# Attended values turned by products with a picking matrix, experts chosen by integer comparison from PSUM

## What is computed

```python
y = state_space_mixer(layernorm(x))                  # chunks, 4 heads, gate, rms norm
x = layernorm(x + (x + y @ W_out))
q, k, v = (x @ Wq.T + bq), (ctx @ Wk.T + bk), (ctx @ Wv.T + bv)   # 16 heads of 8
atten = softmax(q k^T / sqrt(8));  x = layernorm(x + (atten v) @ Wo.T + bo)
logits = x @ gate;  w, e = top_k(logits, 2)          # 8 experts
x = layernorm(x + sum_k softmax(w)_k * (silu(x @ w0[e_k]) * (x @ w1[e_k])) @ wo[e_k])
```

## Time and profile before

| | |
|---|---|
| median of 3 runs | 509.08 us (508.83 to 510.47) |
| the profiled execution | 508.15 us, span of its instructions 506.8 us |
| granted TensorE clock, mean | 0.748 |
| busy PE / DVE / ACT / POOL | 377.8 / 304.8 / 227.5 / 244.4 us |
| span by parts | front and mixer to 80 us, attention to some 302, its tail and the table to 338, experts to 484, end to 507 |

### The profile page before, as it was taken

One profiled execution on the slowest core, in us unless ns is written; L12 is line 12 of the kernel. 1 busy time (PEld: TensorE's weight loads), 2 busy tenths in 40 slices (PEclk: granted clock), 3 DMA queues, 4 the chain that ended last, 5 costly groups with the idle time before them and its releaser, 6 DMA issues.

```text
span 506.8 us, 7843 instructions
## 1 busy us (share of the span) xinstructions
PE 377.8 (75%) x2473; PEld 254.6 (50%) x2473; DVE 304.8 (60%) x778; ACT 227.5 (45%) x455; POOL 244.4 (48%) x309
## 2 busy tenths in 40 slices
PE   3997687877898788787576968218997898888900
PEld 1765555554444465443233424116886687676800
DVE  2655346786768878888987374413545455364635
ACT  2775544124656654646373732013534354353504
POOL 3723676443333415135566665534564555553316
PEclk9997557555759886957675555557899899998975
DMA  8731316355040404161232310011111111111052
GB/s 289 279 107 63 95 52 174 87 137 156 25 136 4 126 4 126 35 179 57 63 118 63 119 42 13 12 53 36 33 43 32 40 39 38 41 32 33 22 181 84
DMA packets 40312, 41.42 MB, mean 82 GB/s; under 512 B 5041, under 2 KB 34033, under 8 KB 40273
## 3 DMA queue, kind: packets, MB, share of 16 engines
q1 hardware_dynamic: 35888, 34.06, 22.2%
q0 software_dynamic: 3520, 5.25, 3.9%
q10 hardware_dynamic: 864, 1.61, 0.9%
HBM read 26.91 MB, written 13.73 MB: 80 GB/s over the span
## 4 chain that ended last, share of the span: by engine, by line
PE 48%; DVE 23%; issue 8%; POOL 6%; another core or an unknown queue 5%; ACT 5%; DMA 3%; DVEq 0%; ACTq 0%; POOLq 0%; SPq 0%
PE banks L886 9%; DVE nm L1079 7%; PE banks L794 4%; PE banks L746 4%; PE banks L909 4%; DVE topf L1141 3%; PE banks L694 3%; PE banks L617 3%; PE banks L714 2%; PE banks L898 2%; POOL table_dram L1553 2%; PE banks L737 1%; PE banks L910 1%; PE banks L704 1%
## 5 line engine op out<-in xcount | busy, mean ns | idle before, releaser
L1380 ACT ACTIVATE probs_all<-banks 128x1024 f32<-128x1024 f32 x64 | 65.5, 1023 | 67.7 <-PE banks L746 65.5
L1079 DVE TENSOR_REDUCE nm<-banks 128x4 f32<-128x1024 f32 x64 | 78.0, 1218 | 15.6 <-PE banks L737 14.5
L886 PE MATMUL banks<-w_split,scores_in 128*128 x234 | 68.5, 431 | 3.6 <-DVE scores_in L1223 2.8
L1578 POOL DMA_INDIRECT y_dram<-avT,scatter_u x39 | 38.2, 979 | 59.6 <-DVE avT L1229 53.5
L794 PE MATMUL banks<-probs_all,vals 128*9 128x256 f32 x512 | 55.2, 515 | 2.3 <-DVE avT L1095 1.2
L746 PE MATMUL banks<-scores_in 32*128 32x256 f32 x256 | 42.7, 420 | 16.6 <-DVE nm L1079 14.5
L1210 DVE TENSOR_TENSOR ctx_in<-ctx_in,banks 128x512 f32<-128x512 f32 x39 | 26.7, 684 | 41.1 <-issue 26.4
L886 PEld LDWEIGHTS banks<-w_split,scores_in 128*128 128x128 f32 x234 | 43.9, 203 | 13.5 <-issue 6.3
L909 PE MATMUL banks<-w_split,scores_in 128*128 x156 | 42.4, 349 | 8.1 <-DVE scores_in L1216 7.7
L737 PE MATMUL banks<-scores_in 32*128 32x256 f32 x256 | 42.4, 418 | 6.2 <-DVE nm L1079 6.0
L1571 POOL DMA_INDIRECT scores_in<-x_dram,gather_i x39 | 37.4, 959 | 18.0 <-issue 11.6
(11 more groups left out here) (212 smaller groups left out, 785.5 us busy)
## 6 DMA issues: line engine op xcount, KB each, us to landing
scores_in<-k_dram SPq DMA_DIRECT2D x32, 128.0 KB, 2.8
scores_in<-q_dram SPq DMA_DIRECT2D x32, 128.0 KB, 3.1
ctx_in<-in_L_ffn_w SPq DMA_DIRECT2D x16, 256.0 KB, 2.6
cs_wide<-cs_dram SPq DMA_DIRECT2D x14, 256.0 KB, 3.7
k_dram<-split_qk SPq DMA_DIRECT2D x8, 256.0 KB, 2.5
q_dram<-split_qk SPq DMA_DIRECT2D x8, 256.0 KB, 2.2
ctx_in<-in_L_ffn_wo SPq DMA_DIRECT2D x8, 256.0 KB, 2.8
x_in<-in_x SPq DMA_DIRECT2D x4, 256.0 KB, 5.2
```

Source lines behind the costliest of these rows:

```text
L886: m = TE.matmul(bank(2 * slot + j), xT[:, i % XT, xh, :], all_weights[:, c + j * FF:][:, bass.ds(expert_at[i], FF)], start=n == 0, stop=n ...
L1079: V.tensor_reduce(most, maxima_of(n).rearrange("p (j k q) -> p j k q", j=2, k=TPS), AX_X, ALU.max, negate=True).then_inc(s["nmax"], 1)
L1380: C.activation(probs(n).rearrange("p j k q -> p (j k q)"), EXPS, ACT.Exp, scale=SCALE).then_inc(s["probs"], 1)
L1578: G.indirect_dma_start(y_dram[:, :], bass.IndirectOffsetOnAxis(ap=scatter_u[:, i:i + 1], axis=0), y_slot[:, i % Y_RING, :], None).then_inc ...
```

## The change

1. `divide` is one stage for the whole batch: eight products with `pick` as moving operand (128x36, one column for each of 9 values of 4 heads) take the place of the eight transposes. Both halves, 2 x 16 heads x 9 values, stand densely in one bank, so DVE divides with one reciprocal of 128x32 and one product of 128x256. `turn_heads` and `out_project` move one step forward for the first six batches.
2. `gate_top`: a product of the identity with the numbers 0 to 7 writes them into the bank beside the logits. DVE compares the integer indices `topi` with that part of the bank; the cast to `topf` is gone. The bank is free with `chosen`, no longer with the copy of the logits.
3. The subtraction into `row_src` moves from DVE to GpSimd, as a stage `choose` of its own behind the wait for `top`.
4. The constant table `rest` gets 36 columns more.

```diff
@@ -73,8 +73,8 @@
 (IDENT, W_IN, LN_W, LN_B, DT_BIAS), N_FIRST = columns(P, DIN, 1, 1, NH)
 (W_K, W_V, B_Q, B_K, B_V), N_KV = columns(D, D, 1, 1, D)
 (ROPE_CS, W_O_MIX, A_LOG), N_MIX = columns(2 * TPS * 2 * ROPE, 2 * D, NH)
-(CAUSAL, BELOW, ABOVE, EXPERT_OFFSET, W_Q, W_O, B_O, D_SKIP, RMS_W, GATE, MASK, LIMIT, CODES, SPARE, IOTA), N_REST = columns(
-    P, P, P, P, D, D, D, NH, 2, NE, NE, 1, B * TOPK * TPS, SLOT_TILES, SLOT_TILES)
+(CAUSAL, BELOW, ABOVE, EXPERT_OFFSET, W_Q, W_O, B_O, D_SKIP, RMS_W, GATE, MASK, LIMIT, CODES, SPARE, IOTA, PICK), N_REST = columns(
+    P, P, P, P, D, D, D, NH, 2, NE, NE, 1, B * TOPK * TPS, SLOT_TILES, SLOT_TILES, GJ * (HD + 1))
 Y_RING = 6
 
 
@@ -158,13 +158,12 @@
     (lambda b: (("gate_top", b), ("choose", b)), 9),
     (whole("split_x2"), 8),
     (whole("x2_norm"), 7),
-    (whole("out_project"), 6),
-    (whole("turn_heads"), 5),
-    (half("divide", 1), 3),
-    (half("divide", 0), 2),
+    (whole("out_project"), 5),
+    (whole("turn_heads"), 4),
+    (whole("divide"), 2),
     (half("evacuate", 1), 0),
 )
-SOONER = (15, 9, 7, 6, 5, 4, 3, 2, 0)
+SOONER = (15, 9, 7, 6, 5, 4, 2, 0)
 BANKS_END = (2, 3)
 LAST_AFTER = 16
 LAST_MIXER = tile_step(NT - 1) + LAGS[0][1]
...
@@ -318,7 +317,6 @@
         logit = sb("logit", [P, TPS, NE])
         top = sb("top", [P, TPS, 8])
         topi = sb("topi", [P, TPS, 8], U32)
-        topf = sb("topf", [P, TPS, 8])
         choice = sb("choice", [P, TOPK, TPS, NE])
         chosen = sb("chosen", [P, TPS, NE], BF16)
         before_b = sb("before_b", [P, P], BF16)
@@ -455,11 +453,13 @@
         def maxima_of(n):
             return bank(6, 2) if second_slot(n) else MAXIMA
 
-        def follow_up(b, half=0):
-
-            if b < B - len(BANKS_END):
-                return MISC
-            return bank(0) if b == B - 1 and half else bank(BANKS_END[b - B])
+        def follow_up(b):
+
+            return MISC if b < B - len(BANKS_END) else bank(BANKS_END[b - B])
+
+        def by_head(b):
+
+            return follow_up(b)[:, 0:TPS * AH * (HD + 1)].rearrange("p (k h c) -> p k h c", k=TPS, c=HD + 1)
 
         def shared(i):
 
@@ -591,15 +591,11 @@
             misc, mix_bank = Bank(q), Bank(q)
             misc.freed_at(s["fall"], TURNED_SUMS)
             ends = [Bank(q) for _ in BANKS_END]
-            last_half = Bank(q)
             for e in ends:
                 e.freed_at(s["nmax"], NPAIR)
-            last_half.freed_at(s["probs"], NPAIR)
-
-            def freed(b, half=0):
-                if b < B - len(BANKS_END):
-                    return misc
-                return last_half if b == B - 1 and half else ends[b - B]
+
+            def freed(b):
+                return misc if b < B - len(BANKS_END) else ends[b - B]
 
             def turn_normed(t):
                 slot = t % 2
@@ -797,17 +793,19 @@
                 if k == 1:
                     m.then_inc(s["av_mm"], 1)
 
-            def divide(b, half):
+            def divide(b):
                 q.wait_ge(s["av_lo"], b + 1)
                 q.wait_ge(s["av_hi"], b + 1)
-                freed(b, half).wait()
-                for g in range(4):
-                    m = TE.transpose(follow_up(b, half)[:, g * P:(g + 1) * P], avT[:, g * S + half * P:g * S + (half + 1) * P], ident)
+                freed(b).wait()
+                for k in range(TPS):
+                    for r in range(GR):
+                        m = TE.matmul(by_head(b)[:, k].rearrange("p (j r) c -> p r j c", r=GR)[:, r],
+                                      avT[:, r * S + k * P:r * S + (k + 1) * P], pick, start=True, stop=True)
                 m.then_inc(s["heads_t"], 1)
-                freed(b, half).freed_at(s["o_norm"], TPS * b + half + 1)
+                freed(b).freed_at(s["o_norm"], b + 1)
 
             def turn_heads(b):
-                q.wait_ge(s["o_norm"], TPS * b + 2)
+                q.wait_ge(s["o_norm"], b + 1)
                 freed(b).wait()
                 for k in range(TPS):
                     m = TE.transpose(follow_up(b)[:, k * P:(k + 1) * P], o_sb[:, k, :], ident)
@@ -834,9 +832,10 @@
                 freed(b).wait()
                 q.wait_ge(s["x2T"], b + 1)
                 for k in range(TPS):
-                    m = TE.matmul(follow_up(b)[:, k * NE:(k + 1) * NE], x2T[:, k * P:(k + 1) * P], gate[:, :], start=True, stop=True)
-                m.then_inc(s["gate_mm"], 1)
-                freed(b).freed_at(s["logit"], b + 1)
+                    TE.matmul(follow_up(b)[:, k * NE:(k + 1) * NE], x2T[:, k * P:(k + 1) * P], gate[:, :], start=True, stop=True)
+                TE.matmul(follow_up(b)[:, TPS * NE:(TPS + 1) * NE], ident, iota[:, 0:NE],
+                          start=True, stop=True).then_inc(s["gate_mm"], 1)
+                freed(b).freed_at(s["chosen"], b + 1)
 
             def rank_chosen(b):
                 q.wait_ge(s["chosen"], b + 1)
@@ -1090,20 +1089,19 @@
             def evacuate(b, half):
                 if half:
                     q.wait_ge(s["av_mm"], GR * (b + 1))
-                    q.wait_ge(s["heads_t"], TPS * b)
+                    q.wait_ge(s["heads_t"], b)
                     q.wait_ge(a["init_dram"], INIT)
                     V.tensor_copy(avT[:, BANK:], AV).then_inc(s["av_hi"], 1)
 
-            def divide(b, half):
-                av = follow_up(b, half).rearrange("p (r j c) -> p r j c", r=GR, c=32)
-                q.wait_ge(s["heads_t"], TPS * b + half + 1)
-                q.wait_ge(s["o_norm"], TPS * b + half)
-                own.step(V.reciprocal(rec[:, :].rearrange("p (r j) -> p r j", r=GR), av[:, :, :, HD]))
+            def divide(b):
+                av = by_head(b).rearrange("p k h c -> p (k h) c")
+                q.wait_ge(s["heads_t"], b + 1)
+                q.wait_ge(s["o_norm"], b)
+                own.step(V.reciprocal(rec[:, :], av[:, :, HD]))
                 own.settle()
                 q.wait_ge(s["o_t"], b)
-                V.tensor_tensor(o_sb[:, half, :].rearrange("p (j r d) -> p r j d", r=GR, d=HD), av[:, :, :, 0:HD],
-                                rec[:, :].rearrange("p (r j) -> p r j", r=GR).unsqueeze(3).to_broadcast([P, GR, GJ, HD]),
-                                ALU.mult).then_inc(s["o_norm"], 1)
+                V.tensor_tensor(o_sb[:, :, :].rearrange("p k (h d) -> p (k h) d", d=HD), av[:, :, 0:HD],
+                                rec[:, :].unsqueeze(2).to_broadcast([P, TPS * AH, HD]), ALU.mult).then_inc(s["o_norm"], 1)
 
             def out_project(b):
                 q.wait_ge(s["wo_mm"], b + 1)
@@ -1127,24 +1125,20 @@
 
             def gate_top(b):
                 q.wait_ge(s["gate_mm"], b + 1)
-                V.tensor_copy(logit[:, :, :].rearrange("p t e -> p (t e)"), follow_up(b)[:, 0:TPS * NE]).then_inc(s["logit"], 1)
-                q.wait_ge(s["logit"], b + 1)
+                own.step(V.tensor_copy(logit[:, :, :].rearrange("p t e -> p (t e)"), follow_up(b)[:, 0:TPS * NE]))
+                own.settle()
+                q.wait_ge(s["gap"], b)
                 for k in range(TPS):
                     own.step(V.max(top[:, k, :], logit[:, k, :]))
                 own.settle()
                 for k in range(TPS):
-                    own.step(V.max_index(topi[:, k, :], top[:, k, :], logit[:, k, :]))
-                own.settle()
-                q.wait_ge(s["consts_g"], ROWS_SET)
-                V.tensor_tensor(row_src[:, b, :, :, 1], top[:, :, 1].unsqueeze(1).to_broadcast([P, TOPK, TPS]),
-                                top[:, :, 0].unsqueeze(1).to_broadcast([P, TOPK, TPS]), ALU.subtract).then_inc(s["gap"], 1)
-                own.step(V.tensor_copy(topf[:, :, :], topi[:, :, :]))
-                own.settle()
+                    V.max_index(topi[:, k, :], top[:, k, :], logit[:, k, :]).then_inc(s["top"], 1)
 
             def choose(b):
+                q.wait_ge(s["top"], TPS * (b + 1))
                 for k in range(TOPK):
-                    own.step(V.tensor_tensor(choice[:, k], iota[:, 0:NE].unsqueeze(1).to_broadcast([P, TPS, NE]),
-                                             topf[:, :, k].unsqueeze(2).to_broadcast([P, TPS, NE]), ALU.is_equal))
+                    own.step(V.tensor_tensor(choice[:, k], follow_up(b)[:, TPS * NE:(TPS + 1) * NE].unsqueeze(1).to_broadcast([P, TPS, NE]),
+                                             topi[:, :, k].unsqueeze(2).to_broadcast([P, TPS, NE]), ALU.is_equal))
                 own.settle()
                 q.wait_ge(s["rank_mm"], b)
                 V.tensor_tensor(chosen[:, :, :], choice[:, 0], choice[:, 1], ALU.add).then_inc(s["chosen"], 1)
@@ -1166,7 +1160,7 @@
             def place_chosen(b):
                 q.wait_ge(a[f"slots{b % 2}"], 16 * TOPK * TPS * (b // 2))
                 V.scalar_tensor_tensor(place_u[:, b % 2].rearrange("p (k t) -> p k t", k=TOPK),
-                                       topf[:, :, 0:TOPK].rearrange("p t k -> p k t"), float(T),
```

(8 more changed lines are left out.)

12 lines of the change are left out of this document (6 added, 6 removed).

## The result

The changed kernel is slower: 511.86 us (median of 4) against 508.95 for the kernel before beside it, ratio 1.0135 with a 95% interval of 1.0072 to 1.0198. On another chip it is 491.16 against 479.06, ratio 1.0257 (1.0207 to 1.0308). On most of them, as on that one, the part with the experts, behind 340 us, takes some 25 us less than on the first, in every kernel alike, while the stretch up to 300 us takes the same. So each time is compared only with the kernel before on its own chip, and kernels on different chips by their distance from it. One kernel's times spread with its granted clock (the change's own from 489.37 at 0.722 to 494.11 at 0.700), so medians have 1 to 3 us of play.

The account below looks back on a forecast made before the run. PE and DVE were taken to bound the middle part by turns, with three stalls. The terms 4.55 + 1.35 - 9.15 - 1.5 + 2.1 gave -2.65 us, so 506.4 us against 509.08, range 500 to 513.

Parts of the forecast that it names:

- rival 2: Divisions: products at half clock throughout, added PE work on the chain at that price, moved step brings nothing; 512.0 us, chance 0.22.
- Bound and stalls: Batches 3 to 5: PE's 14.4 us wait for `o_sb`, blamed on the cast, goes with cast and gaps; -9.15 us.
- Rival 1: Three stalls move to `chosen`, which loses at every border of POOL's row as the cast did; 524 us, chance 0.07.
- Price of the products: Each batch's division: sixteen passes at 0.225 us at half or 0.125 at full clock, so 3.6 or 2.0 us.
- Early divisions, +4.55: Divisions of b=0 to 3, before the stalls: products in place of transposes add 0.95, 0.85, 1.25 and 1.5 us.
- Extra product, +1.35: Gate of b=0, 1, 2: two more passes writing the experts' numbers, 0.45 us each at half clock; +1.35 us.
- Moved steps, -1.5: Turning and out-projection one step forward take DVE work from a late step, for b=3 and partly b=4; -1.5 us.
- Tail, +2.1: Chain through b=7 after the last scores: dearer products, gate of b=6, POOL's subtraction, less DVE time; +2.1 us.
- Rival 3: From about 270 us the full clock returns, where it had stayed at 0.50 to the attention's end; 497 us, chance 0.13.

Follow-up runs that it names:

- one stray copy: Kernel before with the change's routing, transposes kept, plus a copy of the indices directly behind `chosen`: ratio 1.0034; with the copy ahead of the comparisons instead: 1.0021.
- the pair of added products: Kernel before with new routing and moved steps, transposes kept, plus 32 products of 36 columns (481.28 us, ratio 1.0031) or of 128 columns (471.57 us, 0.9864).
- the transposing kernel: Kernel before with the change's routing, eight transposes kept: 468.46 us, ratio 0.975; with the moved steps as well: 463.54 us, ratio 0.9643.
- division alone: Changed kernel with the old routing (cast and gap subtraction on VectorE, choice from SBUF, no extra product): median 487.06 us, ratio 1.0059.
- the wide products: Kernel before with new routing and moved steps, transposes kept, plus two products of 128 columns ahead of each half's transposes: 471.57 us, ratio 0.9864.
- the doubled transposes: Kernel before with new routing and moved steps, each half's four transposes done a second time: 465.96 us, ratio 0.9741; on another chip 0.9663.
- the routing part: Kernel before with the choice from the bank, gaps on GpSimd and the gate's extra product, transposes kept: 468.46 against 479.45 us, ratio 0.975.
- the one-pass products: Changed kernel with the division's products reading only upper halves as bf16, one pass in place of four: 462.50 against 481.32 us, ratio 0.9614.

## Why the prediction was wrong

It said 506.4 us and faster; 511.86 lies in its range and on rival 2's 512.0, to which it gave 0.22. By its terms:

- **Bound and stalls.** The wait of 14.4 us was real, and is gone; -9.15 became -8.3. Its cause was only half told, and `chosen` was safe for another reason than mine: as the only such instruction in the row. Rival 1 was one stray copy away.
- **Price of the products.** 3.6 and 2.0 us for a division measured 3.63 and 1.98. This size was right. The reading behind it, that 8 columns cost as much as 64, set a price at half clock beside one at full; at half clock a pass took 0.21 us with 8 columns, 0.23 with 36 and 0.26 with 128 (2.05 us for eight).
- **Early divisions, +4.55: the step that failed.** It reads "the longer stretch of busy PE reaches the full clock", for b=1 and b=2. The clock did not come: it stayed at 0.50 from 174 to 186 us, though PE was busy for 11.6 of these 12 us, the projections behind the two divisions took 2.05 and 2.06 us where 0.91 was counted on, and the granted clock of 180 to 240 us fell from 0.78 to 0.64. The delay grew by 1.1, 3.3, 2.8 and 2.4 us in the steps of b=0 to 3, together 9.6, where 0.95, 0.85, 1.25 and 1.5 were forecast; the excess lies in b=1 and b=2. Step 42 is 9.1 us late where 4.55 + 1.35 - 1.5 = 4.4 was forecast. That the clock stayed away because the added work had few columns is inferred from the pair of added products; no run has the division itself with more columns.
- **Extra product, +1.35**: perhaps too small, but not settled. By the medians 4.6 us between the changed kernel and the same without it, and 2.6 in the transposing kernel, on different chips each time; exponential 42 is 9.1 us late with it and without it (division alone).
- **Moved steps, -1.5**: in the changed kernel the move costs 0.8 us by the medians, which the spread covers; in the transposing kernel it is worth 4.5, each against the kernel before on its chip.
- **Tail, +2.1**: 2.25.
- **Rival 3** did not come in the change (0.61 in 240 to 300, before 0.59). That a higher clock can be granted there the wide products and the doubled transposes showed, with 0.78 and 0.81. Its "against", that busy time alone did not bring the clock back, held: the changed kernel had 0.61 with PE busy for 52.9 of 60 us.
- **What I did not ask** is what the division alone does to the stall. It removes it too; the gain was booked once, which is right for the sum, but the routing part then had nothing left to earn, and brings a product of its own.

So rival 2's mechanism is shown: the one-pass products take the whole loss away. That columns make a difference to the clock is shown for work added to the transposing kernel, by the pair of added products; for the division's own products it is carried over from there.

## What to carry over

Where two edits remove one wait, time each alone: the cheaper one is enough. Before exchanging transposes for products with a narrow right side, count passes and columns: here such passes cost their full time and some clock besides (24 us of work, 25 to 31 of time). Of DVE instructions that touch only SBUF, leave at most one beside an unbroken row of GpSimd's, and let the others read a bank.

## What the runs showed of the hardware

- Beside an unbroken row on GpSimd, the first DVE instruction of the tried kinds with all operands in SBUF waits for one of its instructions (0.53 to 1.26 us; up to 1.64 in the third place, where an indirect DMA stood ahead of the row), the second for the row's end (4.24 to 5.75 us): cast, copy, addition and comparison alike, also with bank readers between them.
- 32 products of 36 columns and 32 of 128 columns behind 128x128 weights took 15.3 and 15.4 us, and left a granted clock of 0.56 and 0.78 in the same stretch. The Trainium skill, "TensorE: Matmul & The Clock Gate", section "What's actually happening", sets the clock by how busy PE has been. Here the kernel that was busier in that stretch (55.7 of 60 us against 49.8, the same work taking longer at the lower clock) had the lower clock; the trace does not agree with that rule, and the measurement decides.
- 64 more transposes on PE cost about 3 us of the kernel's time by the medians (12.7 below the kernel before on its chip, against 15.5 on another), and PE's busy time in the span fell from 364.2 to 360.1, with the mean granted clock up from 0.769 to 0.796.
